# Local stack: the mask written into PSUM by ScalarE instead of by TensorE, and the second feed-forward chunk in another PSUM pair

## The reference

```python
def look(t):                                   # the window before, and the own one
    p = jnp.pad(t, ((0, 0), (0, 0), (1, 0), (0, 0), (0, 0)))
    return jnp.concatenate([p[:, :, :nw], p[:, :, 1:]], axis=3)
mask = (it < jb) | (it > jb + w) | (jb == -1)
sim = jnp.einsum('bhwie,bhwje->bhwij', bq, bk2) * QK_SCALE      # windows of 32, 16 heads of 64
sim = jnp.where(mask, -jnp.finfo(sim.dtype).max, sim)
attn = jax.nn.softmax(sim, -1)
...
for i in range(DEPTH):                                          # DEPTH = 6
    x = attn_layer(shift_tokens(x), Wqkv[i], q_scale[i], k_scale[i], Wo[i]) + x
    x = ffn_layer(shift_tokens(x), ln_g[i], ln_b[i], W1[i], b1[i], W2[i], b2[i]) + x
```

## Time and profile before

| | |
|---|---|
| median of 3 runs | 4958.59 us (4957.13 to 4967.54) |
| the profiled execution: its own time | 4963.93 us |
| its span, first to last instruction | 4962.1 us |
| granted TensorE clock, mean of the span | 0.935 |
| local stack, first and last score product | 699 to 4131 us |
| one `b` of the local stack | about 72 us |

### The profile page before, as it was taken

One profiled execution on the slowest core, in us unless ns is written; L12 is line 12 of the kernel. 1 busy time (PEld: TensorE's weight loads), 2 busy tenths in 40 slices (PEclk: granted clock), 3 DMA queues, 4 the chain that ended last, 5 costly groups with the idle time before them and its releaser, 6 DMA issues. The chain is left out here.

```text
span 4962.1 us, 116892 instructions
## 1 busy us (share of the span) xinstructions
PE 4540.5 (92%) x46384; PEld 2667.8 (54%) x46384; DVE 3541.4 (71%) x3746; ACT 2295.9 (46%) x3418; POOL 2443.8 (49%) x3467
## 2 busy tenths in 40 slices
PE   5999869999999999999999999999999995588896
PEld 2233346666666666666666666666666663222223
DVE  4777467787777777777777777877777784477763
ACT  0566534444444444444444444444444442055564
POOL 1111056665666666666566666666666661221210
PEclk7999979999999999999999999999999997589997
DMA  2322032222222222222222222222222221122210
GB/s 52 62 54 61 3 98 55 59 60 64 69 63 53 57 73 68 55 59 63 72 57 63 54 69 69 59 53 59 63 63 57 60 59 47 34 53 53 52 28 19
DMA packets 181061, 281.67 MB, mean 57 GB/s; under 512 B 58032, under 2 KB 79792, under 8 KB 174896
## 3 DMA queue, kind: packets, MB, share of 16 engines
q1 hardware_dynamic: 180880, 279.24, 23.7%
HBM read 61.70 MB, written 17.56 MB: 16 GB/s over the span
## 5 line engine op out<-in xcount | busy, mean ns | idle before, releaser
L958 DVE SCALAR_TENSOR_TENSOR l_t<-l_r,l_qkvec,l_tab 128x1024 f32<-128x1024 f32 x768 | 933.3, 1274 | 31.4 <-ACT l_sq L871 28.9
L477 DVE TENSOR_REDUCE a_nmax<-a_pair 128x2 f32<-128x1024 f32 x512 | 609.4, 1220 | 262.7 <-PE a_pair L559 262.5
L395 ACT ACTIVATE a_pt<-a_st 128x512 f32<-128x512 f32 x1024 | 541.8, 604 | 284.8 <-PE a_st L543 279.5
L909 ACT ACTIVATE l_p<-l_p 128x1024 f32<-128x1024 f32 x192 | 203.1, 1058 | 644.8 <-DVE l_p L1015 644.8
L805 POOL TENSOR_TENSOR l_ntmp<-l_seed 128x32 f32<-128x32 f32 (+1 forms) x480 | 110.7, 231 | 788.5 <-ACT l_seed L860 769.4
L832 POOL TENSOR_TENSOR l_u<-l_t 128x512 f32<-128x512 f32 x384 | 491.0, 1279 | 0.0
L833 POOL TENSOR_TENSOR l_u<-l_t 128x512 f32<-128x512 f32 x384 | 490.6, 1277 | 0.0
L1207 PE MATMUL l_r<-l_pbd,l_va 128*64 128x160 f32 (+1 forms) x6144 | 444.3, 298 | 48.0 <-DMA l_pbd<-l_pt 48.0
L838 POOL TENSOR_TENSOR l_p<-l_p,l_srec 128x1024 f32<-128x1024 f32 x192 | 365.1, 1901 | 221.4 <-DVE l_srec L1036 183.3
L1117 PE MATMUL l_r<-xs,l_wqkv 128*128 (+1 forms) x768 | 430.4, 672 | 42.1 <-DVEq L935 23.4
L1207 PEld LDWEIGHTS l_r<-l_pbd,l_va 128*64 128x64 f32 x6144 | 398.5, 138 | 110.0 <-issue 110.0
(11 more groups left out here) (184 smaller groups left out, 7562.7 us busy)
## 6 DMA issues: line engine op xcount, KB each, us to landing
l_kbd<-l_kn SPq DMA_DIRECT2D x1536, 64.0 KB, 2.0
l_pbd<-l_pt SPq DMA_DIRECT2D x1344, 64.0 KB, 2.0
a_ks<-a_scr SPq DMA_DIRECT2D x96, 192.0 KB
a_qs<-a_scr SPq DMA_DIRECT2D x288, 64.0 KB
a_scr<-a_parts SPq DMA_DIRECT2D x48, 256.0 KB, 2.5
l_pbd<-l_pt SPq DMA_DIRECT2D x192, 56.0 KB, 2.0
l_wqkv<-in_wqkv SPq DMA_DIRECT2D x6, 1536.0 KB, 7.4
l_wo<-in_wo SPq DMA_DIRECT2D x6, 512.0 KB, 3.9
```

The costliest lines, as they stand in the source:

```text
L395: nc.scalar.activation(pt[n % 2][:, r, :], st[(4 * n + r + par) % 3][:], ACT.Exp, scale=SC).then_inc(exp_done, 1)
L477: nc.vector.tensor_reduce(out=nmax[:, n, 2 * i:2 * i + 2], in_=pair[i][:], op=ALU.max, axis=AX.X, negate=True).then_inc(pair_dve[i], 1)
L958: last = nc.vector.scalar_tensor_tensor(out=t[a][:, 2 * half:2 * half + 2, :], in0=R[a][:, half, :].unsqueeze(1).to_broadcast([D, 2, T]), ...
```

## The change

TensorE no longer writes the mask. ScalarE copies it (bf16, 128 x 1024) into `R[3]`, and the score products add onto it. For that nothing in `R[3]` may start a new sum, so the sums of squares (and, but for the last body, the variance) are added onto zeros, which ScalarE writes into 2 x 32 columns of `R[3]` as soon as VectorE has taken the scores out, ahead of exp. The copy of the mask stands between the squares of q and the squares of k in steps 0 to 2, and after the seeds of the variance in step 3. Since the second feed-forward chunk starts a new sum too, it goes to `R[1]`.

```diff
         def _(act):
             act.sem_inc(S["sq_free"], 1)
+            act.wait_ge(S["r3_touched"], 2)
+            nc.scalar.activation(R[3][:, :, 0:NSS], zeros[:], ACT.Copy).then_inc(S["r3_cleared"], 1)
@@
+                def place_mask():
+                    nc.scalar.activation(R[3][:], mask[:], ACT.Copy).then_inc(S["mask_placed"], 1)
@@
                             nc.scalar.activation(sq[0][:, half, :], R[0][:, half, :], ACT.Square).then_inc(S["q_dve"], 1)
+                    if c < 3 and live(c, 2, b, prev):
+                        place_mask()
+                    if b is not None:
                         for half in range(2):
                             act.wait_ge(S["k_act"], seen.next(S["k_act"]))
@@
                         seeds(NSS, NSS + NT, S["normv_ready"], S["seedv_ready"])
+                    if c == 3 and live(c, 2, b, prev):
+                        place_mask()
@@
                         act.wait_ge(S["t_ready"], seen.next(S["t_ready"]))
+                        if b is not None:
+                            nc.scalar.activation(R[3][:, :, 0:NSS], zeros[:], ACT.Copy).then_inc(S["r3_cleared"], 1)
                         nc.scalar.activation(p[:], p[:], ACT.Exp, scale=QK_SCALE).then_inc(S["p_ready"], 1)
@@
-                            nc.scalar.activation(hid[i][0:n, :], R[(2, 3, 0)[i]][0:n, 0, :], ACT.Gelu,
+                            nc.scalar.activation(hid[i][0:n, :], R[(2, 1, 0)[i]][0:n, 0, :], ACT.Gelu,
@@ TensorE
+            for bank in range(2):
+                nc.tensor.matmul(R[3][:, bank, :], C["inv"][:], xs[:, bank, 0:T], start=True, stop=True).then_inc(S["r3_touched"], 1)
@@
                                 last = nc.tensor.matmul(R[3][:, 0, o:o + CH], sqs[a][:, 128 * k:128 * k + 128], block4[:],
-                                                        start=True, stop=True)
+                                                        start=False, stop=True, skip_group_check=True)
@@
                     if live(c, 2, b, prev):
-                        claim(3, "r3_dve")
+                        claim(3, "r3_cleared" if b is not None else "r3_dve")
                         pe.wait_ge(S["qn_ready"], seen.next(S["qn_ready"]))
                         pe.wait_ge(S["kbd_full"], seen.next(S["kbd_full"], 2 * CH * 16))
-                        for bank in range(2):
-                            nc.tensor.matmul(R[3][:, bank, :], ident16[:], mask[:, bank, :], start=True, stop=False, skip_group_check=True)
+                        pe.wait_ge(S["mask_placed"], seen.next(S["mask_placed"]))
@@
-                            r = R[(2, 3, 0)[i]]
-                            claim((2, 3, 0)[i])
+                            r = R[(2, 1, 0)[i]]
+                            claim((2, 1, 0)[i])
```

More of the change, by code:

```diff
@@ L679, in local_stack @@
         mask = sb("mask", [D, 2, T], BF16)
-        ident16 = sb("ident16", [D, D], BF16)
         block4 = sb("block4", [D, CH])
+        zeros = sb("zeros", [D, 2, NT * 2 * CH])
         xc = sb("xc", [D, T])
@@ L712, in local_stack @@
                  "r2_act r0_dve r1_dve r3_dve rq_ready ra_ready sq_sum sq_ready ss_ready norm_read norm_ready seed_ready rn_ready var_ready normv_read normv_ready seedv_ready rnv_ready rnx_ready b_ready r0_dve_b "
-                 "qn_ready kn_ready kbd_full s_ready t_ready p_ready rec_ready pn_ready pt_ready pt_free pbd_free "
+                 "mask_placed r3_touched r3_cleared qn_ready kn_ready kbd_full s_ready t_ready p_ready rec_ready pn_ready pt_ready pt_free pbd_free "
                  "va_ready pv_ready ot_ready wo_ready x_ready mean_ready centred fsq_ready bc_ready xng_ready "
@@ L866, in body @@
                         seeds(0, NSS, S["norm_ready"], S["seed_ready"])
+                        if not live(c, 2, b, prev):
+                            nc.scalar.activation(R[3][:, :, 0:NSS], zeros[:], ACT.Copy).then_inc(S["r3_cleared"], 1)
                     if b is not None:
@@ L926, in _ @@
         def _(v):
+            nc.vector.memset(zeros[:], 0.0)
             nc.vector.memset(seed_bias[:], BITS_BIAS).then_inc(S["seed_init"], 1)
@@ L929, in _ @@
             nc.vector.tensor_copy(mask[:], p[:].rearrange("p a b -> p (a b)").rearrange("p (a b) -> p a b", a=2))
-            nc.vector.tensor_copy(ident16[:], C["ident"][:])
             for i in range(2):
@@ L1016, in body @@
                                                 ALU.subtract).then_inc(S["t_ready"], 1)
-                        nc.vector.engine_nop().then_inc(S["r3_dve"], 1)
+                        if b is None:
+                            nc.vector.engine_nop().then_inc(S["r3_dve"], 1)
                     def scale_by_norm(a):
@@ L1043, in body @@
                                 v.wait_ge(S["gelu_ready"], seen.next(S["gelu_ready"]))
-                                nc.vector.scalar_tensor_tensor(out=hid[i][0:n, :], in0=R[(2, 3, 0)[i]][0:n, 1, :],
+                                nc.vector.scalar_tensor_tensor(out=hid[i][0:n, :], in0=R[(2, 1, 0)[i]][0:n, 1, :],
                                                                scalar=vec[0:n, 5 + i:6 + i], in1=hid[i][0:n, :],
@@ L1066, in _ @@
             pe.wait_ge(S["consts_pe"], 16)
-            due = {0: [], 1: [], 2: [], 3: []}
+            for bank in range(2):
+                nc.tensor.matmul(R[3][:, bank, :], C["inv"][:], xs[:, bank, 0:T], start=True, stop=True).then_inc(S["r3_touched"], 1)
+            due = {0: [], 1: [], 2: [], 3: ["r3_cleared"]}
             def body(par, l, start, b, prev):
@@ L1104, in sums_of_squares @@
                                 last = nc.tensor.matmul(R[3][:, 0, o:o + CH], sqs[a][:, 128 * k:128 * k + 128], block4[:],
-                                                        start=True, stop=True)
+                                                        start=False, stop=True, skip_group_check=True)
                         last.then_inc(S["ss_ready"], 1)
-                        due[3] = ["norm_read"]
+                        due[3] = ["norm_read"] if live(c, 2, b, prev) else ["norm_read", "r3_cleared"]
                     if has_ss and c < 3:
@@ L1142, in body @@
                             last = nc.tensor.matmul(R[3][:, 1, k:k + 1], fsq[:, 128 * k:128 * k + 128], C["inv"][:, 0:1],
-                                                    start=True, stop=True)
+                                                    start=(b is None), stop=True, skip_group_check=True)
                         last.then_inc(S["var_ready"], 1)
@@ L1229, in body @@
                     if c == 3 and prev is None:
-                        for i in (0, 2, 3):
+                        for i in (0, 1, 2):
                             read(i)
```

## The result

The changed kernel takes 4917.9 us (median of 4 runs, 4903.9 to 4924.4) against 4957.9 for the kernel before: ratio 0.9913, interval 0.9893 to 0.9932, so 0.9% faster. The forecast was 4910. The profiled execution has a span of 4922.6 us, where that of before had 4962.1.

A forecast was written before the change was run, and what follows sets the result against it. TensorE, 92% busy, was taken to wait on other engines, DMAs and settle in four places, with clock falls besides. Terms averaged -1.04 us a b, -49 us over 47: 4958.6 to 4910 us, range 4888 to 4935.

The forecast's parts named there:

- The mask products: TensorE, from mask start to scores: each removed pair saves 0.53 us, 102 us at most over 192 pairs.
- Which steps count: Per b: 0.53 us gained in steps 0 and 2, none in step 1 without a fall; step 3 only with a fall.
- The clear: ScalarE ahead of exp: delays exp and row sum by about 0.15 us, twice in a b with a step 1 fall.
- The mask on ScalarE: Copy of 1.01 to 1.06 us, hidden in all steps: cost 0; without cover 1.0 us a b, 47 us.
- The second chunk: Step 3, feed-forward: waits 0.7 us for the copy out of R[1], next product 0.35 us later; bounds 0.1 to 0.7.
- The sum: Change per b: -0.71 us without a fall, -0.94 with one in step 1, -1.24 with one in step 3; mean -1.04.
- The falls: Drops of TensorE's granted clock to 0.50, about 1.2 us each, most b's having one; the sum left their number unchanged.
- rival 3: The clock falls less often: half of the falls gone are 25 us more, all 50, 4885 to 4860; 13 in 100.
- rival 5: Slower: new TensorE waits bring a second fall in each b, 1.74 us each, 78 us in all, 4988; 15 in 100.
- Rival 2: TensorE is the bound everywhere and the waits give way: -102 us, 4857; 9 in 100.
- Rival 4: ScalarE eats most of it: clear 0.25, feed-forward 0.7; +0.1 us a b without a fall, 4949; 13 in 100.

The follow-up runs named there:

- e4: Kernel before with the two mask products left out and nothing put in, so scores are not masked; ratio 0.9909 to the kernel before.
- e9: Changed kernel without the clear, and with +50 everywhere in place of the mask; ratio 0.9914 to the kernel before.
- e5: Changed kernel with a clear of 256 columns in place of 64; ratio 0.9971 to the kernel before.
- e6: Changed kernel with one more ScalarE copy of the mask, to SBUF, ahead of the real one; ratio 0.9946 to the kernel before.
- e3: Kernel before with the second feed-forward chunk in R[1] and nothing else; ratio 1.0016 to the kernel before.
- e7: Changed kernel with, in step 3, ScalarE's copy out of R[1] ahead of the clear and exp; ratio 0.9888 to the kernel before.
- e10: Changed kernel with the clear behind exp instead of ahead of it; ratio 0.9976 to the kernel before.
- e1: Kernel before, unchanged, run and profiled once more; ratio 1.0006.
- e8: As e7, and TensorE's settle moved from behind the third feed-forward chunk to behind the first; ratio 0.9958 to the kernel before.

## Why the prediction was right

The direction, the size within 8 us and the mechanism held. That the number came so near is in part luck: the mask products and the second chunk were both priced too high, one as a gain and one as a loss, and two changes in the falls of the clock that the sum had at nothing cancelled (below).

**The mask products: mis-sized.** I took 0.53 us for a pair; it is 0.43 (e4, and the step from the v products to the scores, 2.25 to 1.82). The distance from the mask's start to that of the scores holds 0.10 us that stays when the mask goes, since the step to the scores is 0.31 from whatever product of 0.216 stands ahead. The row ahead of the mask shows it in the kernel before: the eight v products, of 256 columns in fp32, start 1.72 ahead of the mask, so 0.215 each. The Trainium skill ("TensorE: Matmul & The Clock Gate", Back-to-back issue gap) had 0.43 for two by its figure for a single product, and the 0.216 us measured agree with it. The same section gives about 131 ns for products of 512 columns in a sustained stream; no row here comes near that.

**Which steps count: right.** e4 lost 0.83 in a `b` without a fall (two masks), 1.33 with one in step 3 (three), 1.29 with one in step 1 (three), and without a fall in just the stretches named: 1 to 2 and 3 to the next 0. The covers were where the rows put them: L1028 waits 0.64 us in step 0 (1.08 - 0.43), L1194 0.76 for GpSimd (0.31 + 0.43).

**The clear: right in place, a little small in size.** No cost without a fall, 0.38 in a `b` with a fall in step 1 (e9), where I had 2 x 0.15. The way from step 0 to 1 stayed free by little: the argument left out that the transpose of the softmax, which the clear delays, had only about 0.15 us in hand against SP's queue, just what the clear took (e5).

**The mask on ScalarE: right, 0.** Steps 0 to 3 take in the changed kernel what they take in e4, which has neither mask nor copy (14.25, 17.50 and 17.30 against 14.27, 17.50 and 17.29). e6 added 0.95 us a step and lost 0.22 a `b`.

**The second chunk: mis-sized.** I charged 0.35; from step 3 to the next step 0 the changed kernel loses 0.19 against e4 (20.89 and 20.70). The hole was as forecast (0.64), but it fills time that `settle` had left open: alone it costs some 0.05 there (e3), and taking it away gives 0.02 (e7). The other part came with the changed kernel. Its last feed-forward product starts 7.73 to 7.75 us behind the first chunk, as in e6, e7, e9 and e10 (7.73 to 7.77), where before, e1, e3 and e4 have 7.59; what the former have and the latter don't is the semaphore of the placed mask, one more in `settle`. That it is this semaphore, at a spacing of 0.15, fits all of these rows, but it was not tried by itself.

**The sum.** Without a fall -0.68 (forecast -0.71); in step 3 -1.16 (-1.24); in step 1 -0.75 (-0.94).

**The falls: the assumption that missed.** I left their number as it was. In the two profiles of before, 63 of 70 `b`s have one; in those of after 45 of 70, and 7 of these are of a kind that before did not have and that costs 3.65. So rival 3 and the mechanism of rival 5 both came true in part. At the prices of the changed kernel, the single falls that are gone save 0.38 us a `b`, 18 us in all, and the seven long ones cost 0.37, 17 us in all. They cancel, and nothing in the rows of before said that they would. The mean of the 35 moved by -0.93 (71.82 to 70.89), forecast -1.04. Over 47 `b`s, -0.93 would be -44. The first two `b`s of a layer gain less (75.88 to 75.17 in the mean of ten), and the start of the stack is 2.9 us longer (two fp32 products to touch `R[3]`, from 652.17 to the next product at 655.74, which no term of mine had). That gives 36 - 3 = 33 us in the profiles; the runs say 34 to 53 (the first interval). Of the difference I can only say that unchanged stages scatter by 10 to 20 us from one execution to the next.

**Rival 2** is refuted by e4: with no mask at all and nothing in its place, 0.9% is gained, not 2%. **Rival 4** is refuted by the lengths without a fall (-0.68, where it had +0.1). **Rival 5** did not decide here, but it does in e8 and e10: there a kernel whose `b` without a fall is within 0.2 and 0.01 us of the changed one's is 0.4% and 0.6% slower than it by the ratios. In their profiles falls came more often (e10) or where TensorE had nothing to wait for (e8), and that fits the size: the mean of the 35 is 0.4 to 0.5 us longer in e10 and 0.7 to 0.8 in e8, of which its length without a fall is 0.16.

## What to carry to other kernels

A removed instruction is worth its time only in the rounds in which its engine comes last: count those rounds from the waits behind it, and price it between the row ahead and the row behind. A new wait in front of an engine that another delay holds up anyway (here a chain of semaphore instructions on TensorE's queue) can cost nothing, so look for what holds the next step before charging it. And where a loop has a fall of the clock in some rounds and not in others, compare the rounds with and without a fall apart, and take the count of falls as a risk of some tenths of a per cent that any move of a wait can turn.

## What the hardware showed beyond that

- A fall of the clock has a price that depends on its place: 1.65 to 1.70 us at the beginning of step 0, where TensorE has no slack (e5, e8); 1.2 in step 1 and 1.3 in step 3 of the kernel before, 1.15 and 0.85 in the changed one; and with a fall in step 1 and a long one in step 3 3.65.
- Equal lengths do not give equal falls. The changed kernel and e10 have the same `b` without a fall (69.95 us) and the same with one in step 1 (71.09), but of 35 `b`s the one has four with more than one fall and the other ten, with three each. The differences seen are that some 0.6 us of idle time lies ahead of the sums of squares rather than behind them, and that VectorE's rows behind exp come 0.15 sooner; which of them decides was not tried.
- 22 semaphore instructions of 51 ns each on TensorE's queue take 3.2 us, 0.15 from one to the next, and hold up the products behind them: put behind the first chunk, they made the second wait 0.53 us (e8).
